# Cross-attention and a low-rank mixture: attended halves read back to be scaled, and the mixture's scaling given to VectorE

## What is computed

```python
# attention: q = layernorm(x), k = v = ctx; each of the 4 x 8 heads is a block of 128 rows
qk  = einsum('bhdq,bhdl->bhql', qh, kh) / sqrt(128)
ret = einsum('bhql,bhdl->bhdq', softmax(qk), vh)
x   = x + gamma * ret
# mixture, with n = layernorm(x); K = 8 experts of rank R = 64
h     = relu(einsum('bsd,de->bse', n, W1) + b1)
alpha = softmax(einsum('bse,ek->bsk', h, W2) + b2)
vx    = einsum('krd,bsd->bskr', V, n)
uvx   = einsum('kdr,bskr->bskd', U, vx)
x     = x + einsum('bsk,bskd->bsd', alpha, uvx)
```

## Time and profile before

| | us |
|---|---|
| three runs, median | 1560.44 |
| lowest to highest | 1558.99 to 1562.46 |
| the profiled execution | 1564.22 |
| its span, first to last instruction | 1562.4 |
| first matmul of the mixture | at 782.8 |
| busy: PE / DVE / POOL / ACT | 1490.6 / 1012.5 / 886.4 / 824.2 |
| mean granted TensorE clock, of full speed | 0.993 |

### The profile page before, as it was taken

How to read it: one execution, slowest core, us unless ns; L and a number is a source line. 1 busy time by engine, 2 the same in 40 slices (tenths; PEclk the granted TensorE clock), 3 DMA queues, 4 the chain that set the end, 5 groups by cost and what they waited for, 6 DMA issues and landing times.

```text
span 1562.4 us, 20458 instructions
## 1 busy us (share of the span) xinstructions
PE 1490.6 (95%) x6216; PEld 1145.7 (73%) x6216; DVE 1012.5 (65%) x1237; ACT 824.2 (53%) x1266; POOL 886.4 (57%) x520
## 2 busy tenths in 40 slices
PE   5989999999999999999779999999999999999999
PEld 3666777777777777777557877778777787877877
DVE  7999999999999999999556334333443334433212
ACT  5877898888989898898732222111221122111120
POOL 2889888888898888888733243432523335233200
PEclk9999999999999999999899999999999999999999
DMA  5898889899998998998874553645436454454403
GB/s 162 277 287 278 267 274 289 268 278 279 279 276 268 289 272 276 278 278 251 296 267 124 168 173 121 224 135 185 164 111 213 139 183 161 135 201 134 135 1 108
DMA packets 142085, 332.19 MB, mean 213 GB/s; under 512 B 29152, under 2 KB 48864, under 8 KB 142048
## 3 DMA queue, kind: packets, MB, share of 16 engines
q1 hardware_dynamic: 124480, 284.01, 58.6%
q10 hardware_dynamic: 17568, 47.72, 8.9%
HBM read 134.26 MB, written 48.50 MB: 117 GB/s over the span
## 4 chain that ended last, share of the span: by engine, by line
PE 75%; DVE 10%; ACT 4%; DMA 3%; POOL 3%; issue 2%; SPq 2%; ACTq 0%; DVEq 0%; POOLq 0%
PE scores L1062 18%; PE scores L558 17%; PE attended L580 13%; PE attended L1124 10%; PE attended L583 5%; PE scores L1106 5%; PE spare L1106 4%; DVE ht_lo L1204 3%; DVE pb L622 2%; DVE neg_max L613 2%; POOL pt_lo L338 1%; PE scores L1077 1%; DMA attended_rows<-att_out 1%; ACT hidden L1006 1%; ACT ht_hi L1009 1%
## 5 line engine op out<-in xcount | busy, mean ns | idle before, releaser
L338 POOL TENSOR_TENSOR pt_lo<-pt,pt_hi 128x512 fp32r<-128x512 f32 (+1 forms) x256 | 478.4, 1883 | 96.6 <-ACT pt_hi L408 95.5
L429 ACT ACTIVATE probs<-scores,neg_max 128x1024 f32<-128x1024 f32 x256 | 285.5, 1115 | 98.7 <-DVE neg_max L613 98.5
L613 DVE TENSOR_REDUCE neg_max<-scores 128x1 f32<-128x1024 f32 x256 | 309.1, 1207 | 27.2 <-PE scores L558 26.9
L622 DVE STREAM_TRANSPOSE pb<-probs 128x1024 f32<-128x1024 f32 x256 | 315.3, 1231 | 16.9 <-DMA pt<-pb 8.3
L558 PE MATMUL scores<-k_hi,q_hi 128*128 128x512 f32 x512 | 209.2, 490 | 20.5 <-ACT probs L429 11.0
L1006 ACT ACTIVATE hidden<-scores,b_col 128x512 f32<-128x512 f32 x64 | 44.2, 690 | 347.9 <-PE scores L1062 347.9
L1204 DVE TENSOR_TENSOR ht_lo<-hidden,ht_hi 128x512 fp32r<-128x512 f32 x64 | 76.9, 1201 | 227.2 <-ACT ht_hi L1009 227.2
L408 ACT ACTIVATE pt_hi<-pt 128x512 fp32r<-128x512 f32 (+1 forms) x256 | 214.4, 837 | 0.0
L1062 PE MATMUL scores<-nt_hi,w_hi 128*128 128x512 f32 x512 | 200.8, 392 | 0.0
L965 POOL TENSOR_TENSOR first_n<-first_n,gain_wide 128x1024 f32<-128x1024 f32 x28 | 81.4, 2907 | 210.4 <-DMA first_n<-attended_rows 193.5
L1062 PE MATMUL scores<-nt_hi,w_lo 128*128 128x512 f32 x512 | 200.2, 391 | 0.0
(11 more groups left out here) (107 smaller groups left out, 2585.5 us busy)
## 6 DMA issues: line engine op xcount, KB each, us to landing
pt<-pb SPq DMA_DIRECT2D x512, 256.0 KB, 5.2
result<-x SPq DMA_DIRECT2D x64, 256.0 KB, 4.3
out<-result SPq DMA_DIRECT2D x64, 256.0 KB, 3.0
k_raw<-in_ctx ACTq DMA_DIRECT2D x30, 512.0 KB, 5.3
x_raw<-in_x ACTq DMA_DIRECT2D x30, 512.0 KB, 6.4
attended_rows<-att_out SPq DMA_DIRECT2D x56, 256.0 KB, 5.2
gain_wide<-gains SPq DMA_DIRECT2D x28, 512.0 KB, 3.7
x_wide<-in_x SPq DMA_DIRECT2D x28, 512.0 KB, 4.6
```

The costliest lines, as they stand in the source:

```text
L338: nc.gpsimd.tensor_tensor(pt_lo[2 * parity + half][:, :, keys, :], pt[2 * parity + half][:, :, keys, :], as_f32(hi[half][q][:]), ALU.subtr ...
L429: nc.scalar.activation(probs[j % 2][:], scores[j % 2][:], ACT.Exp, bias=neg_max[:, j:j + 1], accum_out=row_sum[b][:, j:j + 1]).then_inc(s_ ...
L613: nc.vector.tensor_reduce(neg_max[:, j:j + 1], scores[j % 2][:], AX_X, ALU.max, negate=True).then_inc(s_max, 1)
L622: nc.vector.transpose(pb[half][:, :, j % HALF, :], probs[j % 2][:]).then_inc(s_blocks, 1)
```

## The change

1. **Early heads.** Heads 0 to 3 are stored to `attended_rows` like the others. In heads 3 to 10, one half i = 0 to 7 each, SP fetches the gain row, reads the half back into a tile of its own (`own_half`), loads half of x; DVE scales at step 7, POOL adds at step 7 behind its value split, and SP stores the half to x1 in the next head. Eleven heads after head 0 are written out in place of seven.
2. **Where attention ends.** SP stores what is due before it loads the first tiles, and loads two of them only behind the next gather. PE's turning of the first tiles comes one step later, and ACT's work is ordered anew. Two of the last four low parts of the probabilities go from POOL to DVE (`low_probs_end`).
3. **Mixture.** `scale_and_add` moves from POOL to DVE, in the steady groups before ht_lo of blocks 1, 2, 6 and 7. In group 0 tiles 0 and 1 have it before blocks 2 and 3, tiles 2 and 3 behind the softmax. In group 0 the low parts of V and U move from DVE to POOL, with new places for all high parts. SP loads the attended tiles first, in group 0 before the last attended store has landed. The router products of block e stand behind 18 matmuls of block e + 1 in place of 12; those of block 7 stay.

```diff
@@ attention
+    OWN_AT = 3
+    def own_at(h):
+        return h - OWN_AT if isinstance(h, int) and OWN_AT <= h < OWN_AT + 2 * FIRST else None
-        for h in range(1, FIRST + 4):
+        for h in range(1, OWN_AT + 2 * FIRST + 1):
@@ sync
+        def load_own(i):
+            b = i % 2
+            rows = bass.ts(i // 2, P)
+            sp.wait_ge(s_gain_out[b], i // 2 * 16 + 16)
+            sp.wait_ge(s_scaled, i)
+            sp.dma_start(gain_row[:], scratch[bass.ds(i, 1), :].rearrange("a n -> (a n)")
+                         .partition_broadcast(P)).then_inc(s_gain_in, 16)
+            sp.wait_ge(s_att[b], i // 2 * 16 + 16)
+            if i >= 2:
+                sp.wait_ge(s_own_out[b], i // 2 * 16)
+            sp.dma_start(own_half[b], att[rows, b * BANK:(b + 1) * BANK]).then_inc(s_own_in[b], 16)
+            sp.wait_ge(s_added, i)
+            sp.dma_start(x_half[:], x[rows, b * BANK:(b + 1) * BANK]).then_inc(s_res_in, 16)
@@ sync, slot
-            if last:
-                load_first(n)
             if not (known and h < 3):
                 store_attended(h - 3, 1)
-            if known and 2 <= h < FIRST + 2:
-                spread_gain(h - 2, 1)
-                load_residual(h - 2, 1)
+            if last:
+                load_first(n, (0, 1))
             if not first:
                 send_gain(h - 1, 1)
+            if own_at(h - 1 if known else h) is not None:
+                store_own(own_at(h - 1))
+            if own_at(h) is not None:
+                load_own(own_at(h))
             gather(h, n, 0, parity)
+            if last:
+                load_first(n, (2, 3))
@@ vector, first groups' low parts of the probabilities
+            if u == 6:
+                low_probs_end(1)
+            if u == 7:
+                low_probs_end(3)
             low_first(u)
@@ mixture
+    W1_AT = ((1, 2), (3, 4, 5), (6,), (7,), (), (), (), ())
+    VU_AT = ((), (), (8,), (9,), (10, 11), (12, 13), (14, 15), ())
@@ gpsimd
+            if first:
+                for n in range(KB, KB + 6):
+                    low_weights(n)
+                factor(g, 0)
+                low_weights(KB + 6)
+                factor(g, 1)
+                low_weights(KB + 7)
+                factor(g, 2)
+                factor(g, 3)
@@ tensor
-                issue_all(big[:12] + (router_products(g, e - 1) if e else []) + big[12:])
+                issue_all(big[:18] + (router_products(g, e - 1) if e else []) + big[18:])
@@ vector
+        def hidden_stage(g, e):
+            if e == 1:
+                scale_and_add(g, 0)
+            if e == 2:
+                scale_and_add(g, 1)
+                measure(g, 0)
+            if e == 3:
+                measure(g, 1)
+                normalise(g, 0)
...
+            if e == 6:
+                scale_and_add(g, 2)
+            if e == 7:
+                scale_and_add(g, 3)
+        def first_hidden_stage(g, e):
+            for n in W1_AT[e]:
+                low_weights(n, dve)
+            if e == 2:
+                scale_and_add(g, 0)
+            if e == 3:
+                scale_and_add(g, 1)
+                measure(g, 0)
+            if e == 4:
+                measure(g, 1)
+                normalise(g, 0)
...
             softmax(g)
             if not last:
-                statistics(g, 2)
-                dve.wait_ge(s_stat, g * (2 * GT) + 6)
+                if first:
+                    scale_and_add(g, 2)
+                    scale_and_add(g, 3)
+                measure(g, 2)
```

200 lines of the change are left out of this document (105 added, 95 removed).

## The result

The changed kernel takes 1565.92 us (median; 1564.66 to 1568.06), the kernel before, run beside it, 1561.09: ratio 1.0026, 95% interval 1.0015 to 1.0038. It is 4 us slower; the prediction said 19 us faster, 1541, with 1552 as its upper end. The profiled execution of the changed kernel took 1568.06 us (span 1566.3), 3.8 more than that of before (1564.22), so the two traces can be set against each other.

What follows compares the result with a forecast made beforehand. TensorE bounds the kernel, busy 1490.6 of 1562.4 us. Terms 4.4 + 6.0 + 17.6 + 0.4 - 9.0 = 19.4 us won bring the profiled 1564.2 to 1544.8, median 1541; range 1533 to 1547 (0.53), wider 1527 to 1552.

Steps and rivals of the forecast that it cites:

- own heads: Attention's early heads: one scaling and addition a head over eight heads costs 8.8 us against 13.2, 4.4 won.
- end of attention: Where attention ends: the store ahead of the loads ends ACT's wait; 6.0 us won, bounds 3 and 8.
- groups 1 to 6: Mixture's steady groups: ht_lo no longer held up by POOL; 17.6 us won, bounds 14 and 20.
- group 0, hidden: Group 0's hidden stage: today's 14.8 us loss gives way to new waits and half clock of 14.4; 0.4 won.
- group 0, logits: Group 0 behind the logits: late scaling of tiles 2 and 3 stalls expert products 4.9 and 2.6, clock 1.5; 9.0 lost.
- I take 1.1, nearer to the full share, since DVE and POOL no longer hold each other: Early heads: each own head costs 1.1 us over a steady one, between bounds 0 and 3.3.
- The next load or gather takes over: End of attention: another load or gather becomes the next wait, the lower bound of 3 us won.
- ACT's 5.63 us go: End of attention: ACT's wait for a store vanishes; PE's, POOL's and ACT's chains restart up to that much earlier.
- over a microsecond: Groups 1 to 6: the slack left before the router product asks for ht_lo, for the first two tiles.
- SP's order makes it dear: Group 0 behind the logits: tile store and four result loads precede alpha's store; first gating at 25.7 against 16.6.
- rival (a): Group 0 and early heads: VectorE's scalings and additions wait out POOL passes; 6 us less gain, 1547; chance 0.12.
- Rival (b): Early heads: DMA sets the pace at 26.0 us each, 13.2 lost, 1559; chance 0.06 at 1557 or more.

Runs made afterwards that it cites:

- mix_mended: Changed kernel with four mixture mends: rstd early, tiles 2 and 3 before the softmax, tile 0 and gain row first, gain row before U; 1535.30 us, 0.9830 of before.
- tiles_early: Changed kernel, in group 0 tile 2 scaled in block 7 and tile 3 before the softmax, not both behind it; 0.9958 of the kernel before.
- best: mix_mended plus own transfers behind gather and attention store, end store before loads, block 3's W1 low part and statistics behind ht_lo; 1533.59 us, 0.9826 of before.
- port_apart: mix_mended, but in group 0 POOL's first two low parts of V wait until VectorE has scaled and added tiles 0 and 1; 0.9854 of the kernel before.
- own_no_x: Changed kernel, but the half of x for early halves is loaded once, not eight times; eleven heads take 12.9 us over steady ones.

## Why the prediction was wrong

| term of the sum | predicted | in the two traces | what the runs showed |
|---|---|---|---|
| own heads | 4.4 won | 0.6 lost | 13.0 and 13.4 us over steady heads in two traces with old heads, median 13.8 in nine with new |
| end of attention | 6.0 won | 2.9 won | a wait of 3.45 us in place of 5.63, and another store behind the moved loads; 3.2 more when it is moved |
| groups 1 to 6 | 17.6 won | 12.6 won | 4.2 more with the gain row sooner, 5.9 in mix_mended |
| group 0, hidden | 0.4 won | 5.7 lost | rstd's place alone 14.8 of the stage |
| group 0, logits | 9.0 lost | 12.3 lost | tiles' place alone 11.2 |

All five terms missed on the same side, 22.5 us in all, and the first hidden block came 0.7 us earlier where I had named 10; a further 1.2 us was lost in steady heads (387.4 us from the fifteenth key split to the last, 386.2 before), where the mechanisms of the change do nothing and other kernels with the same attention have 385.5 to 387.2.

**Own heads.** The failed step is "I take 1.1, nearer to the full share, since DVE and POOL no longer hold each other". The measured price is 1.7 a head, between the bounds 0 and 3.3. The DMA share did rise to 0.95, as supposed, and the price stayed. VectorE (22.7 to 23.4 of 24.2 us busy) and the DMA engines are both close to full; that they hold the head between them fits the five kernels with something left out, but is not shown. Spreading eight equal pieces over more heads wins only if their price falls with the load, and it didn't: 1.7 us a half either way.

**End of attention.** "The next load or gather takes over" was my lower bound of 3, and it is what came. The failed step is "ACT's 5.63 us go": I followed the store that was moved, not the loads that it overtook, whose statistics now hold ACT for 3.45 us at the same place, nor the next store, which the edit puts behind two loads (3.39 us).

**Groups 1 to 6.** The mechanism was right: ht_lo is 0.69 in all 64 cases, the wait for POOL is gone. I looked for the rest at the third tile and "over a microsecond" was to be left for the first two. It was the reverse. I counted the chain from gain row to gain row (3.9 us), but not the first gain row, issued at the group's start behind two tiles of 512 KB and waited for 3.5 us, nor the statistics ahead of the low part.

**Group 0, hidden stage.** Places and culprits were right, sizes weren't. TensorE's three waits add up to 14.3 us where I had 11.8, and the rest of the 20.5 us over group 7, 6.2, is mostly half clock behind three waits, where I had 2.6 behind two. Block 2 came 6.2 us late by its interval (12.17 against 5.94), where I had 2: a wait of 4.5 us, in which the gain row landed late behind U and POOL's pass stretched the addition from 1.23 to 3.19, and a half clock that I had not put in at all. Block 4 came as counted: 6.5 us late, and I had 5.5 and 1.3 for the clock. Block 5 was 6.5 us late too, where I had 3.0 and 1.3: rstd ended 5.3 us behind the block's `hidden` (831.09), as counted, but VectorE's normalising took 2.75 beside POOL in place of 0.81. So two passes stretched by POOL, which the sum had at nothing, are 3.9 us of this stage. (The terms that I wrote down for the two rstd chains and for the first gating add up to 9.25, 6.75 and 25.35, not 9.4, 6.9 and 25.7; that is small beside the misses.)

**Behind the logits.** "SP's order makes it dear" was right in direction: the first gating came 28.3 us behind hidden(7) (878.16 against 849.84), where I had 25.7. The missing 2.6 are mostly the alpha store's landing: 4.8 us from issue to spread, behind a tile's store and four loads, where the earlier trace rows had 2.05 with free queues. TensorE's two waits became one of 7.9 us and one of 0.6, 8.5 in all where I had 7.5; the other 3.8 of the 12.3 are mostly half clock, for which I had 1.5. tiles_early shows that with the scaling early SP's order costs a microsecond at most.

**The port.** My rival (a) was a third of 17 us. The Trainium skill, SBUF — State Buffer, section "Who interferes with whom", says that of a VectorE pass with two SBUF inputs and a GpSimd pass that reads SBUF the later one waits for the whole of the first. The rows agree: 1.99 us alone, 4.22 beside a POOL pass of 2.48 that began 0.15 sooner. In the changed kernel the stretched addition of block 2 and the stretched normalising of block 5 stand right before ht_lo and cost 2.0 and 1.9 us; so (a) came true in group 0, with 3.9 us of the 22.5 missed, too small a part to be the cause. With rstd and the tiles in other places the port still stretches passes (mix_mended, best), and port_apart doesn't tell what they cost. Rival (b), the DMA engines set the pace, had the sign of the own heads' miss; own_no_x shows that a transfer less a head brings under 1 us; whether they set it together with VectorE is not shown. No rival had the chains of group 0 longer than I counted them, nor the half clock behind them, and group 0, 18.0 us lost where I had 8.6, is what made the kernel slower.

## What to carry to other kernels

Work that moves between engines brings its waits along: before the move is priced, follow each new waiter back to the DMA issue and to what is queued ahead of it, for the first piece as well as for the steady one. Here 29 us lay in three orders (a tiny factor behind six large passes, two scalings behind a softmax, a row of gains behind 1 MB); a fourth, a row of gains behind 2 MB, only moved its stall to the next block when mended. With these mended the same move is 27 us faster than the kernel before. And work that is spread thinner need not get cheaper: with VectorE and the DMA engines both near full a half cost 1.7 us at two a head and at one a head.

## What was not expected of the hardware

The hold between VectorE and GpSimd also takes one-tensor passes: the normalising, a TENSOR_SCALAR over 1024 columns, took 0.81 us alone (826.34 in the changed kernel) and 2.11 to 2.75 beside a POOL subtraction. The Trainium skill says in the same section that tensor_scalar can enter a two-port mode, if its operands meet some conditions, and then contends with GpSimd; these rows agree. A store of 16 KB (alpha) took 4.8 us from its issue to the spread that waits for it, behind 1.5 MB of other transfers, 2.05 without them; a gain row behind U's 2 MB 6.9 us. And nine kernels with the same attention heads differ in the own heads alone by up to 4 us (12.8 to 16.8, one trace each), as much as most of the differences that the experiments on these heads show.
